# Two tiles in turn on VectorE in the attention step, and the last unit's rows in a place of their own

## The reference, cut to what matters

```
x = x + norm(encoder(norm(x)))     # 4 layers of linear attention (16 heads of 16) and a feed-forward net of 4 D
x = x + norm(mix(norm(x)))         # softmax gate over 8, base product + low-rank parts
x = x + norm(mamba(norm(x)))       # conv of 4, silu, 16 states, 512 channels, over rows of 512 tokens
x = x + norm(experts(norm(x)))     # 8 experts, top 1, at most 320 tokens each

def linear_attention(q, k, v):     # qp = elu(q) + 1, kp = elu(k) + 1
    kv = einsum('bshd,bshm->bhmd', kp, v)
    ksum = sum(kp, axis=1)
    z = 1.0 / (einsum('blhd,bhd->blh', qp, ksum) + 1e-6)
    return einsum('blhd,bhmd,blh->blhm', qp, kv, z)

# mamba: delta = softplus(dt @ W_dt + b_dt), u = silu(conv(x_in)), for each state s and channel d
h = h * exp(delta * A) + (delta * u) * B ; y = sum over s of h * C ; y = (y + u * D) * silu(z)
```

## Time and profile before

| | |
|---|---|
| median of 3 runs | 2807.98 us (2802.28 to 2816.81) |
| profiled execution | 2808.76 us, its span 2807.4 us |
| PE | 2395.0 us busy (85%) |
| DVE | 1837.7 us (65%) |
| POOL | 1720.1 us (61%) |
| ACT | 1617.1 us (58%) |
| granted PE clock | 0.913 of full on average |

### The profile page before, as it was taken

One profiled execution on the slowest core, in us unless ns is written; L12 is line 12 of the kernel. 1 busy time (PEld: TensorE's weight loads), 2 busy tenths in 40 slices (PEclk: granted clock), 3 DMA queues, 4 the chain that ended last, 5 costly groups with the idle time before them and its releaser, 6 DMA issues. The chain is left out here.

```text
span 2807.4 us, 40036 instructions
## 1 busy us (share of the span) xinstructions
PE 2395.0 (85%) x13040; PEld 1959.6 (70%) x13040; DVE 1837.7 (65%) x3883; ACT 1617.1 (58%) x3649; POOL 1720.1 (61%) x1988
## 2 busy tenths in 40 slices
PE   6999998898979868798988887989898766766798
PEld 5889887587859755687877765887797642122598
DVE  4233333678677765878378667784787765979566
ACT  4555656676746555666475665765665556523153
POOL 1011223297659873798369856994598745778356
PEclk8999999999979988899989998999899877788899
DMA  4436233223313232222223133231331232323142
GB/s 159 177 132 219 73 126 123 88 68 99 113 56 107 68 120 88 72 92 86 99 65 113 50 132 94 68 113 62 105 91 43 71 115 86 83 65 95 42 152 95
DMA packets 123898, 273.84 MB, mean 98 GB/s; under 512 B 9213, under 2 KB 64125, under 8 KB 114092
## 3 DMA queue, kind: packets, MB, share of 16 engines
q1 hardware_dynamic: 120108, 263.37, 29.3%
q0 software_dynamic: 3584, 7.92, 0.8%
HBM read 215.93 MB, written 58.48 MB: 98 GB/s over the span
## 5 line engine op out<-in xcount | busy, mean ns | idle before, releaser
L1975 POOL TENSOR_TENSOR sb_sc<-sb_bc,sb_du 128x512 f32<-128x512 f32 x512 | 658.6, 1292 | 106.3 <-issue 35.7
L1988 POOL TENSOR_TENSOR sb_ya<-sb_ya,sb_sc 128x512 f32<-128x512 f32 x384 | 494.9, 1289 | 38.4 <-DVE sb_sc L1233 38.4
L673 PE MATMUL ps<-sb_w,sb_fa 128*128 128x256 f32 x2048 | 489.7, 383 | 4.2 <-ACT sb_fa L1589 4.1
L461 PE MATMUL ps<-sb_hT,sb_w 128*128 128x256 f32 x2048 | 398.1, 295 | 15.8 <-DVE sb_hL L1053 5.9
L1723 ACT ACTIVATE ps<-sb_dl,sb_aneg 128x512 f32<-128x512 f32 x512 | 349.9, 687 | 101.6 <-DVE sb_sc L1233 92.9
L673 PEld LDWEIGHTS ps<-sb_w,sb_fa 128*128 128x128 f32 x2048 | 374.1, 192 | 48.6 <-issue 5.4
L1221 DVE TENSOR_TENSOR_SCAN ps<-ps,sb_sc 128x512 f32<-128x512 f32 x240 | 293.0, 1225 | 93.8 <-ACT ps L1723 89.9
L1221 DVE TENSOR_TENSOR_SCAN ps<-ps,sb_hl,sb_sc 128x512 f32<-128x512 f32 x240 | 307.0, 1283 | 66.5 <-ACT ps L1723 62.7
L461 PEld LDWEIGHTS ps<-sb_hT,sb_w 128*128 128x128 f32 x2048 | 327.3, 193 | 31.9 <-issue 20.3
L1233 DVE TENSOR_TENSOR sb_sc<-ps,sb_bc 128x512 f32<-128x512 f32 x480 | 322.3, 672 | 0.0
L1589 ACT ACTIVATE sb_fa<-ps,sb_b1n 128x256 f32<-128x256 f32 x512 | 209.9, 464 | 142.8 <-PE ps L461 142.5
(11 more groups left out here) (262 smaller groups left out, 5063.1 us busy)
## 6 DMA issues: line engine op xcount, KB each, us to landing
sb_bc<-b_and_c SPq DMA_DIRECT2D x128, 512.0 KB, 5.0
sb_w<-w_parts SPq DMA_DIRECT2D x15, 2048.0 KB, 7.8
sb_wq<-w_qkv_parts SPq DMA_DIRECT2D x15, 1536.0 KB
sb_w<-in_w SPq DMA_DIRECT2D x16, 1024.0 KB
sb_raw<-in_mw SPq DMA_DIRECT2D x16, 1024.0 KB, 8.4
gate_z<-sb_xin SPq DMA_DIRECT2D x30, 256.0 KB, 2.2
sb_zt<-gate_z SPq DMA_DIRECT2D x30, 256.0 KB, 5.5
expert_in<-sb_bb SPq DMA_DIRECT2D x5, 1032.0 KB, 13.3
```

What stands on the lines that cost most here:

```text
L461: ins = pe.matmul(bank, lhs[x], rhs[y], start=(first and m == 0), stop=(last and m == 2), skip_group_check=True)
L673: ins = pe.matmul(acc[:, v * D:(v + 1) * D], fa[i % 3][:, h * 256 + v * 128:h * 256 + (v + 1) * 128], w2[:, 2 * f + h, :], start=(f == 0 a ...
L1975: p.tensor_tensor(db[m % RING], bc[:, i % 3, 0, :], dus[u][:, c, :], ALU.mult).then_inc(S("bm"), 1)
L1988: p.tensor_tensor(yas[u][:, c, :], yas[u][:, c, :], db[m % RING], ALU.add).then_inc(S("ad"), 1)
```

## The change

Four things change.

`attended` on DVE goes over the two tiles of a group in turn: add, add, reciprocal, reciprocal, multiply, multiply, with four `zz` tiles in place of three, and the group's due time is `AT_DVE` = 1.58 after its base in place of 1.02 (the second tile had 0.5 more).

The end of the rates on DVE goes in pairs of channel parts: add, add, multiply, multiply.

Unit 7 has its own `px7`, `pT7`, `xc7`, which lie where the second set of expert weights comes to lie. The load of its rows waits for the encoder's last feed-forward product, no longer for unit 6's rates. The convolution of unit 7 no longer waits until `xc` is read for unit 6. In return the second expert's ACT copy waits for all of `du` and `yi`; it moves to `RATES[1] + 12`, its POOL subtraction to `RATES[1] + 16`, and a weight load of SP to `RATES[1] + 18`. The small copy `dbt` has a new wait for the `wd` products of the unit before.

Tables are set anew: due times by some tenths mostly, the start of unit 5's input (`PRE[5]`) by 12.5, the second silu of every unit by 2. The `WARM_` tables hold 66 more idle matmuls over the whole kernel: in block 1 before the first, second and fourth group of a layer, in block 3 eight before the transposes of the first group, and 12 at the end.

```diff
-PRE = (441.33, 681.85, 1108.84, 1392.06, 1785.49, 2084.25, 2480.86, 2540.0)
+PRE = (441.33, 681.85, 1108.84, 1392.06, 1785.49, 2071.79, 2480.86, 2540.0)
-AT_DVE = 1.02
+AT_DVE = 1.58
...
-WARM_AT = ((4, 4, 0, 0), (4, 0, 0, 0), (4, 0, 0, 0), (4, 0, 0, 0))
-WARM_TR2 = ((0, 0, 1, 0), (0, 0, 1, 0), (0, 0, 1, 0), (0, 0, 1, 0))
+WARM_AT = ((4, 3, 0, 0), (8, 1, 0, 0), (4, 0, 0, 0), (4, 0, 0, 0))
+WARM_TR2 = ((0, 0, 1, 0), (0, 0, 1, 2), (0, 0, 1, 0), (8, 0, 1, 0))
...
-WARM_END = (18, 22, 20, 6, 20, 10)
+WARM_END = (18, 22, 20, 6, 20, 22)
...
-        zz = [sbt(phase1, f"zz{i}", [128, H]) for i in range(3)]
+        zz = [sbt(phase1, f"zz{i}", [128, H]) for i in range(4)]
...
-        e1 = [[sbt(phase2, f"e1{i}{h}", [128, 2, FF], F32R) for h in range(2)] for i in range(2)]
+        e1 = [[sbt(phase2, f"e10{h}", [128, 2, FF], F32R) for h in range(2)]]
+
+        with ExitStack() as late:
+            px7, pT7, xc7 = [sbt(late, name, [128, n, 512]) for name, n in (("px7", 2), ("pT7", 2), ("xc7", 4))]
+        e1.append([sbt(phase2, f"e11{h}", [128, 2, FF], F32R) for h in range(2)])
...
                 for b, l, g in groups:
                     k = place(b, l, g)
+                    yield lay(b, l, BASE_T[kind(b, l)][g] + AT_DVE)
+                    tiles = []
                     for t in range(2):
-                        yield lay(b, l, BASE_T[kind(b, l)][g] + 0.5 * t + AT_DVE)
                         i = 2 * k + t
-                        heads, z = by_head(where["at", i][:, 0:272]), zz[i % 3]
+                        heads, z = by_head(where["at", i][:, 0:272]), zz[i % 4]
                         v.wait_ge(S("at"), i + 1)
-                        n = own.tick(v.tensor_scalar(z[:], heads[:, :, 16], 1e-6, None, ALU.add))
+                        tiles.append((t, heads, z, own.tick(v.tensor_scalar(z[:], heads[:, :, 16], 1e-6, None, ALU.add))))
+                    for t, heads, z, n in tiles:
                         v.wait_ge(S("dve"), n)
                         n = own.tick(v.reciprocal(z[:], z[:]))
-                        v.wait_ge(S("dve"), n)
+                    for t, heads, z, _ in tiles:
+                        v.wait_ge(S("dve"), n - 1 + t)
                         v.tensor_tensor(xh[at(b, g)][:, t, :].rearrange("p (h m) -> p h m", h=H), heads[:, :, 0:16],
                                         z[:].unsqueeze(2).broadcast_to([128, H, 16]), ALU.mult).then_inc(S("an"), 1)
...
-                        if u:
+                        if 0 < u < NU - 1:
                             v.wait_ge(S("yi"), 4 * (u - 1) + c + 1)
-                        elif c == 0:
+                        elif u == 0 and c == 0:
...
-                    for c in range(4):
-                        q = 4 * u + c
-                        yield rates_at(u) + RATE_AT[u][6] + 0.5 * c
-                        v.wait_ge(S("ln"), q + 1)
-                        v.wait_ge(S("m5"), 2 * q + 2)
-                        n = own.tick(v.tensor_tensor(dls[u][:, c, :], dls[u][:, c, :], dus[u][:, c, :], ALU.add))
-                        v.wait_ge(S("dve"), n)
-                        v.tensor_tensor(dus[u][:, c, :], dls[u][:, c, :], xc[:, c, :], ALU.mult).then_inc(S("du"), 1)
+                    for half in range(2):
+                        yield rates_at(u) + RATE_AT[u][6] + half
+                        done = {}
+                        for c in (2 * half, 2 * half + 1):
+                            v.wait_ge(S("ln"), 4 * u + c + 1)
+                            v.wait_ge(S("m5"), 8 * u + 2 * c + 2)
+                            done[c] = own.tick(v.tensor_tensor(dls[u][:, c, :], dls[u][:, c, :], dus[u][:, c, :], ALU.add))
+                        for c in (2 * half, 2 * half + 1):
+                            v.wait_ge(S("dve"), done[c])
+                            v.tensor_tensor(dus[u][:, c, :], dls[u][:, c, :], xcs[u][:, c, :], ALU.mult).then_inc(S("du"), 1)
...
                     if u:
                         e.wait_ge(S("d_bcs"), 16 * u)
+                        e.wait_ge(S("wd"), 4 * u)
                     copy(dbt[:], where["wxm", u][0:96, :]).then_inc(S("db"), 1)
...
             def high_first(n):
                 e.wait_ge(S(f"d_x{2 * n % 4}"), loads(NB, 1) + 16 * (n // 2))
+                if n == 1:
+                    e.wait_ge(S("du"), 4 * NU)
+                    e.wait_ge(S("yi"), 4 * NU)
...
-                yield ahead(35.0)
+                yield RATES[1] + 12.0
                 high_first(1)
...
-                    yield ahead(20.0 + 20.0 * n)
+                    yield RATES[1] + 16.0 if n else ahead(20.0)
                     low_first(n)
...
-                    if u:
+                    if u == NU - 1:
+                        q.wait_ge(S("w2"), 4 * GROUPS)
+                    elif u:
                         q.wait_ge(S("m5"), 8 * u)
```

More of the change, by code:

```diff
@@ L98 @@
 XF = 14.51
-TR = -3.99
+TR = -4.4
 TR_ACT = -3.28
-TR_DVE = -2.18
-SCALE = 0.69
-ADD_PE = 2.06
+TR_DVE = -2.34
+SCALE = 1.0
+ADD_PE = 1.7
 LEAD = 1.98
-BC = -5.45
+BC = -5.49
 EXP = 0.83
@@ L276, in build @@
         db = [sc[:, n, :] for n in range(RING)]
-        ab = [px[:, 2 * c:2 * c + 2, :].rearrange("p t d -> p (t d)") for c in range(2)] + [pT[:, c, :] for c in range(2)]
         by_head = lambda x: x.rearrange("p (h m) -> p h m", m=17)
@@ L735, in unit_input @@
                         where["ptr", 2 * u + k] = bank
-                        ins = transposes(bank, px, [(t, k) for t in range(4)], freed,
+                        ins = transposes(bank, pxs[u], [(t, k) for t in range(4)], freed,
                                          (("lnp_p", 3 * u + 3), ("lna_p", 2 * u + 2)), spare=WARM_IN[u][0] if k == 0 else 0)
@@ L751, in unit_input @@
                         for k in range(2):
-                            ins = pe.matmul(bank[:], wi[:, k, c * 128:(c + 1) * 128], pT[:, k, :],
+                            ins = pe.matmul(bank[:], wi[:, k, c * 128:(c + 1) * 128], pTs[u][:, k, :],
                                             start=(k == 0), stop=(k == 1))
@@ L762, in unit_input @@
                         for k in range(2):
-                            ins = pe.matmul(bank[:], wi[:, k, DIN + c * 128:DIN + (c + 1) * 128], pT[:, k, :],
+                            ins = pe.matmul(bank[:], wi[:, k, DIN + c * 128:DIN + (c + 1) * 128], pTs[u][:, k, :],
                                             start=(k == 0), stop=(k == 1))
@@ L774, in unit_input @@
                     for c in range(4):
-                        ins = pe.matmul(bank[0:96, :], wx[:, c, :], xc[:, c, :], start=(c == 0), stop=(c == 3))
+                        ins = pe.matmul(bank[0:96, :], wx[:, c, :], xcs[u][:, c, :], start=(c == 0), stop=(c == 3))
                     ins.then_inc(S("win"), 1)
@@ L1165, in unit_input @@
                     v.wait_ge(S("d_bx"), 16 * (u + 1))
-                    sums(px, "p", 4)
+                    sums(pxs[u], "p", 4)
                     w = C["convw"]
@@ L1180, in unit_input @@
                                 v.wait_ge(S("dve"), n)
-                            ins = v.scalar_tensor_tensor(out=xc[:, c, :] if k == 2 else where["win", m][:], in0=xi[:, k:k + 512],
+                            ins = v.scalar_tensor_tensor(out=xcs[u][:, c, :] if k == 2 else where["win", m][:], in0=xi[:, k:k + 512],
                                                          scalar=w[:, c, k:k + 1], in1=where["win", m][:],
@@ L1679, in rates @@
                             e.wait_ge(S("d_bh"), 16 * (u + 1))
[L1680 removed]
+                        e.activation(abs_[u][c], where["wd", q][:], ACT.Abs, bias=C["bdt"][:, c:c + 1]).then_inc(S("ab"), 1)
                         e.wait_ge(S("ab"), 2 * q + 1)
[L1682 removed]
+                        e.activation(abs_[u][c], abs_[u][c], ACT.Exp, scale=-1.0).then_inc(S("ab"), 1)
                         if u == LATE:
```

80 lines of the change are left out of this document (41 added, 39 removed).

## The result

The changed kernel takes 2795.77 us (median of 11 runs, 2792.81 to 2802.45) against 2807.59 of the kernel before in the same session (11 runs). The ratio is 0.9965, 95% interval 0.9953 to 0.9977: faster by 0.35 per cent, some 10 us. The time lies where it was forecast. The way to it does not: the attention step gave half of its term, the rates' end several times its own, the new due times gave something where I had nothing, the late part cost where I had a small gain, and the misses cancel.

What follows compares the result with a forecast made beforehand. No engine bounds it throughout: PE in the first block, later PE, POOL and DVE passing short waits. Terms -13.2 - 0.8 - 1.9 + 1.5 + 0.5 = -13.9 from 2808.76 gave 2794.9, stated as 2795; range 2777 to 2812.

Steps and rivals of the forecast that it cites:

- the attention step: Encoder blocks 0 to 3: interleaving saves DVE 0.44 us a group, 1.76 a layer; -1.5, -4.4, -6.8, -0.5, together -13.2 us.
- the rates' end: End of each unit's rates: four multiplies shed 0.1 us each, counting only in units 6 and 7; -0.8 us.
- the new due times: Unit 5's earlier input order and due times moved by under 1.5 us: costed at nothing, may do either.
- the late part: Unit 7's own places and moved expert preparation: earlier load gains nothing, ACT copy -1.9 us, POOL subtract +1.5.
- Whatever DVE saves in front of L982 comes off that wait: Block 2: PE's 4.62 us wait for a layer norm shrinks by DVE's whole saving, 1.7 a layer, -6.8 us.
- Idle matmuls in block 3 end before L1102's result, not after: Sign for block 3's first group: eight idles, 2.1 us, against a wait of 1.81 that some layers have.
- as one piece of 4.5 us it holds up the products of four steps: POOL's subtract among unit 6's last steps, where POOL has 4.8 us free: bounds 0 to +4.5, taken +1.5.
- The first leaves a chain that DVE waits on: -1.9: Unit 7: ACT's expert copy of 1.89 us moves away from where DVE waits for the exponential; -1.9 us.
- The end: Before the experts' transposes: twelve more idles cost 3.8 us, 1.15 covered; bounds -1.5 to +2.6, taken +0.5.
- Nothing: Rival: DVE doesn't overlap operations, or savings return as waits for POOL and PE; 2806 us, chance 0.21.
- Whole gain: Rival: all 1.76 us a layer passes in blocks 1 to 3, idles lie in waits; 2783 us, chance 0.27.
- Slower: Rival: 66 more idles cost PE 17.5 us and the DVE gain stops at POOL; 2823 us, chance 0.12.

Runs made afterwards that it cites:

- late part alone: The kernel before with only unit 7's own places and the moved copy, subtraction and load; 2810.28 us against 2806.23, ratio 1.0015.
- numbers alone: The kernel before with all due times and WARM tables of the changed one, code as before; 2802.47 us against 2806.23, ratio 0.9992.
- without late part: The changed kernel with unit 7 in the shared px, pT, xc and the copy, subtraction and load back in their places; 2790.45 us, ratio 0.9946.
- moved work only: The changed kernel with unit 7 in the shared places, but copy, subtraction and weight load still later; 2794.74 us against 2808.53, ratio 0.9947.
- best: The changed kernel without unit 7's own places and moved work, with 10 idles at the end in place of 22; 2789.29 us, ratio 0.9934.
- the first four: One session: new order alone in the kernel before 2808.66 us, taken out of the changed kernel 2796.20; idle matmuls likewise 2808.57 and 2798.78.

## Why the prediction was right in the number, and where it was wrong

**The attention step: price on DVE right, place wrong.** "Whatever DVE saves in front of L982 comes off that wait, so the 1.7 a layer count in full" was said of block 2. The time between the first `kvm` of one block and of the next says otherwise (us):

| | block 1 | block 2 |
|---|---|---|
| neither edit (4 kernels: before, idles alone, late part alone, numbers alone) | 602.1 to 604.3 | 587.2 to 588.8 |
| new order, no pairs (2) | 594.9, 595.5 | 587.6, 587.9 |
| pairs and numbers, old order (2) | 603.4, 604.1 | 584.8, 581.5 |
| both (4: changed, without late part, moved work only, best) | 595.2 to 597.6 | 584.0 to 585.5 |

The two that are left out have both edits too: with the idles of before 600.4 and 584.8, with the due times of before 600.5 and 587.4. So with one half of the new tables taken out, half or more of block 1's 7 us is gone too (one profile each).

The new order gives 7 us in block 1, where I had put 4.4, and nothing in block 2, where I had put 6.8 (block 3 shows nothing of either edit, as forecast for this one). The stage rows suggest why block 2 keeps none of it. Its second layer, in the kernel before and in the one with the new order alone; columns as in the earlier trace rows:

```profile
1266.60:1406.20 139.60, 128.05 (x722) 108.40 (x722) 82.92 (x205) 80.36 (x192) 78.29 (x101) 0.97 0.25 86
```

```profile
1255.00:1396.60 141.60, 130.09 (x722) 109.77 (x722) 81.43 (x205) 80.60 (x192) 79.72 (x102) 0.95 0.26 86
```

PE is busy 128.05 of 139.60 us and DVE 82.92: I read this layer as PE's, and it lasts 2 us longer at a granted clock of 0.95 than at 0.97, with 1.5 us less of DVE's work. (The 139.6 is the shortest of the 14 profiles, the others have 141.0 to 143.1, so the 2 us themselves say little; that PE sets this layer's length is argued from the busy times, no run shows it.) I had read a wait of 4.62 us for one layer norm as a price on DVE; it got longer instead (5.56 us, ended at 1278.70 in the changed kernel): counted from the `kvm` mark the norm came after 18.9 us in place of 19.9, but PE was there 2 us sooner, and the layer as a whole took 143.0 us in place of 139.6. Block 1, in the kernel before and with the new order alone:

```profile
551.10:1153.50 602.40, 513.49 (x2834) 438.56 (x2834) 433.27 (x876) 366.91 (x851) 436.15 (x477) 0.90 0.28 87
```

```profile
548.60:1144.10 595.50, 501.74 (x2834) 428.99 (x2834) 427.48 (x875) 367.09 (x850) 435.10 (x476) 0.93 0.29 88
```

The same 2834 matmuls take PE 501.7 us in place of 513.5, at a clock of 0.93 in place of 0.90, while its time without work grew from 88.9 us to 93.8. So in this pair nothing came off PE's waits: the whole 6.9 us, and more, is busy time at another clock, and one profile each can't say that the edit brought it. With the new numbers in both kernels (numbers alone, then with the new order) it is otherwise:

```profile
547.10:1149.20 602.10, 509.55 (x2887) 433.90 (x2885) 434.34 (x876) 367.85 (x851) 435.08 (x476) 0.92 0.27 87
```

```profile
550.50:1145.30 594.80, 507.97 (x2886) 434.24 (x2885) 428.48 (x875) 367.77 (x850) 434.24 (x476) 0.93 0.28 88
```

Here PE's time without work falls from 92.6 to 86.8 us and its busy time by 1.6. The other two pairs that differ in the order alone agree: 3.6 us less without work in the changed kernel than in the one without the new order, 5.5 without the late part.

This fits the runs of the new order alone, which shows 7 us in block 1 of its profiled run, its fastest, and nothing in the median of its eleven. One thing stays open: taken out of the changed kernel the new order makes no difference to the median, and taken out of the kernel without the late part it costs 6 to 7 us. Each median is good to about 4 us.

Block 3 shows nothing, as forecast, but not in the way forecast. "Idle matmuls in block 3 end before L1102's result, not after" was a sign, and it came out the other way. The changed kernel's second layer there:

```profile
1843.14 0.75 DVE L1112 TENSOR_TENSOR sb_xh<-ps,sb_zz 128x256 f32<-128x256 f32 x2
...
1845.70 1.95 PE L461 MATMUL ps<-sb_pack 128*128 128x128 f32 x16
1847.49 0.60 PE L455 MATMUL ps<-sb_pack,sb_xh 128*128 128x128 f32 x4
```

DVE had written both tiles at 1843.89, before the eight idles began; in all four layers they stand, for 1.95 to 2.23 us, in front of data that is there. The three layers between this block's marks took 107.7, 141.8 and 115.2 us all the same, against 106.9, 143.7 and 115.9.

**The rates' end: "each of the four sheds 0.1 us, 0.4 a unit" and "Only in units 6 and 7" made -0.8, the term that was mis-sized most for its size.** It is worth 7 us (2797.66 against 2790.45 without the late part, and 7.1 within one session), 3 of them in block 2. One or two more lie between the last `kvm` and unit 7's statistics (195.0 and 193.6 us in the two kernels, 193.0 in the best); where the rest lies the marks don't show. I took the multiply's price from unit 7, 0.69 us. Over all 32 of them the line's summary in the kernel before and its answer in the changed kernel are (shortest, median, longest, in ns):

```profile
L1206 DVE TENSOR_TENSOR sb_du<-sb_dl,sb_xc x32: 691/1632/1658, 537.5 to 2445.7; 128x512 f32<-128x512 f32 x32
```

```profile
L1218 DVE TENSOR_TENSOR sb_du<-sb_dl,sb_xc x32: 676/681/685, 539.9 to 2431.1; 128x512 f32<-128x512 f32 x32
```

More than half of the multiplies took 1.63 us. The timeline of unit 5's rates in the kernel before says when:

```profile
2009.20 0.69 DVE L1206 TENSOR_TENSOR sb_du<-sb_dl,sb_xc 128x512 f32<-128x512 f32 x1
2009.81 0.69 DVE L1204 TENSOR_TENSOR sb_dl<-sb_dl,sb_du 128x512 f32<-128x512 f32 x1
2010.03 1.59 POOL L1975 TENSOR_TENSOR sb_sc<-sb_bc,sb_du 128x512 f32<-128x512 f32 x1 [3.89 <-issue]
2010.53 1.63 DVE L1206 TENSOR_TENSOR sb_du<-sb_dl,sb_xc 128x512 f32<-128x512 f32 x1
```

The first multiply lets POOL start the first product of the steps, and the next multiply runs beside it: 1.63 us in place of 0.69, and POOL's 1.59 in place of the 1.29 that is its mean. Both read two tiles from SBUF. Of the 64 adds and multiplies in this trace, the 19 that start while POOL is at such a product take 1.16 to 1.66 us and the other 45 take 0.68 or 0.69. In unit 7, from where I took my rows, no product of POOL runs beside them: it is the only unit without the effect. In the changed kernel POOL can start only when both adds and the first multiply of a pair are done:

```profile
2001.34 1.28 DVE L1218 TENSOR_TENSOR sb_du<-sb_dl,sb_xc 128x512 f32<-128x512 f32 x2
2002.16 3.27 POOL L1991 TENSOR_TENSOR sb_sc<-sb_bc,sb_du 128x512 f32<-128x512 f32 x2 [4.59 <-issue]
2002.54 1.75 DVE L1215 TENSOR_TENSOR sb_dl<-sb_dl,sb_du 128x512 f32<-128x512 f32 x1
```

Now the second pair's adds meet it, two a unit in five of the first seven units and none in the other two, in place of two or three multiplies in each. In one of those two, unit 4, it is POOL that stands back: its product takes 4.00 us while DVE's second pair goes through at full speed.

```profile
1706.25 4.00 POOL L1991 TENSOR_TENSOR sb_sc<-sb_bc,sb_du 128x512 f32<-128x512 f32 x1 [4.74 <-issue]
1706.63 1.28 DVE L1215 TENSOR_TENSOR sb_dl<-sb_dl,sb_du 128x512 f32<-128x512 f32 x2
1707.84 1.28 DVE L1218 TENSOR_TENSOR sb_du<-sb_dl,sb_xc 128x512 f32<-128x512 f32 x2
```

Up to 2300 us the adds and multiplies took 52.7 us for 53 instructions before and 46.7 for 56 after: 0.99 and 0.83 each, 9 us over 56. The Trainium skill states the contention without a price (GPSIMD Engine Reference, "Specifications": the SBUF interfaces are shared with VectorE, contention with instructions that have two SBUF inputs); the rows agree and put 0.95 us on a multiply of 0.69.

**The late part: -0.4 forecast, +4 to +5 measured.** "as one piece of 4.5 us it holds up the products of four steps. Bounds: 0 to +4.5, I take +1.5" was the right mechanism at a third of its size. DVE and POOL in the changed kernel, among unit 6's last steps; in brackets the idle before, and who ended it:

```profile
2446.81 4.51 POOL L2054 TENSOR_TENSOR sb_e<-sb_raw,sb_e 128x2048 fp32r<-128x2048 f32 x1
...
2452.85 3.77 PE L825 MATMUL ps<-sb_sc,sb_pack 128*128 128x512 f32 x4 [4.86 <-POOL sb_sc L2015]
...
2454.11 1.23 DVE L1233 TENSOR_TENSOR_SCAN ps<-ps,sb_sc 128x512 f32<-128x512 f32 x1 [4.47 <-POOL sb_sc L1991]
```

POOL is 4.51 us away, DVE stands for 4.47 and PE for 4.86. In the list of DVE's waits between 2400 and 2500 us (us, times, longest) the changed kernel, the one without the late part and the one with the moved work alone have

```profile
DVE ps L1233 <- POOL sb_sc L1991: 7.6, 4, 4.5
```

```profile
DVE ps L1229 <- POOL sb_sc L1983: 2.3, 2, 2.1
```

```profile
DVE ps L1229 <- POOL sb_sc L1983: 7.0, 3, 4.5
```

The stretch from the rates' end to unit 6's output took 46.5 to 48.3 us in the six profiled kernels with the moved work and 40.3 to 44.3 in the eight without. The earlier trace rows said it, had I read them to the end: DVE busy 28.3 of 29 us means there is nobody to take up a stop. The other side, "The first leaves a chain that DVE waits on: -1.9", is only seen in part: from the statistics to the rates' end four of the six took 133.6 to 134.8 us, two 136.4 and 137.3, against 136.7 to 139.3 without. Both stretches together took 181.0 to 184.1 us with the moved work and 179.6 to 181.4 without, 2 us apart on average; where the rest of the 4 to 5 lies isn't shown. The own places by themselves gain nothing, as forecast; by the medians the moved work costs 4.1 us and the whole late part 4 to 5, which leaves them little to cost.

**The end: +0.5 forecast, +1.3 measured**, within its bounds. **The due times at nothing:** the numbers alone gave 4 us with an interval that reaches to no change, and taken out of the changed kernel the due times cost 3 to 5. They are worth something; that a step that is free sooner is used sooner only if the next is placed there is my reading, and which of the many numbers does it wasn't separated.

**The rivals.** "Nothing" fell in its first form, that DVE doesn't overlap, with the 1.16 us a group; its second form, that what is saved is given back, is what the new order alone did to its median. "Whole gain" fell in blocks 2 and 3. "Slower", by idles at 0.265 us each, fell to the kernel with the idles alone; the last section has what they brought.

With each term from the pair of kernels that differ in it alone, the sum of -13.9 reads: order -6.5, pairs -7, numbers -4 (with the end's +1.3 in them), late part +5, which is -12.5, each good to about 4 us. The forecast was within a microsecond by luck: the attention step missed by +7 and the late part by +5, the rates' end by -6 and the numbers by -4.

## What to carry to other kernels

A duration belongs to what runs beside it: take the median and the longest of a line over the whole trace, not one row from the stage that looks cleanest, and ask of a line with two levels what the other engines do at the higher one. Work that is put "where an engine has room" can cost about its whole length if it is one piece and the next engine is at 97 per cent, as the 4.5 us did here; look at the busiest neighbour and not at the engine's own share. Independent small operations on VectorE overlap (1.16 us in place of 1.64 here), but what VectorE saves is not what the kernel saves: of 0.48 us a group in 64 groups, 31 us, some 7 arrived, and TensorE's waits in block 1 got shorter in the three pairs of kernels with the new numbers and not in the one without. And a stretch that got shorter in one profile each is to be split into busy time and waiting before a wait is given the credit: here the same 2834 matmuls differed by 12 us.

## What the runs showed of the hardware

Runs of one kernel differ by up to 21 us, and much of the difference goes with TensorE's clock. In 11 runs of the new order alone time and mean granted clock go together with a correlation of -0.93, in the changed kernel's 11 with -0.85, in the 33 of the kernel before beside the first four with -0.67; 0.01 of granted clock (of the 2.4 GHz level) goes with 18, 13 and 14 us. That the clock is the cause isn't shown by this. Kernels with more idle matmuls have a little more of it:

| | runs | mean granted clock | median us |
|---|---|---|---|
| before (beside the first four) | 33 | 0.9205 | 2806.73 |
| idles alone | 12 | 0.9227 | 2808.57 |
| changed | 11 | 0.9240 | 2795.77 |
| changed, idles of before | 12 | 0.9185 | 2798.78 |

Sixty-six more idles take PE about 17 us at 0.265 each, and go with 0.0022 to 0.0055 more of clock, which by the slopes above is 3 to 10 us (an estimate). If the rest of their time lay in waits, they pay for themselves and hardly more, which fits that neither putting them in nor taking them out shows; how much of it lay in waits wasn't measured over the whole kernel, and in block 3 it did not, and at the end only in part.
